# Gated cross-attention: the short path written out as one list, with scores issued further ahead, two buffers for two transposed operands, and one norm chain per batch

## What is computed

```
memory_proj = einsum('bme,de->bmd', memory, W_mem)
scores = einsum('bnd,bmd->bnm', x, memory_proj) / sqrt(D)
context = einsum('bnm,bmd->bnd', softmax(scores), memory_proj)
gate = sigmoid(einsum('bnf,df->bnd', concat([x, context]), W_gate) + b_gate)
x = rmsnorm(x + gate * context, norm_w)            # eps 1e-6
q = (layernorm(x) * ln_q_g + ln_q_b) @ Wq * 64 ** -0.5
k, v = split(ctx @ Wkv)
sim = where(media_mask, q @ k, -huge)              # 16 heads
x = x + tanh(attn_gate) * (softmax(sim) @ v) @ Wo
h = layernorm(x) * ln_ff_g + ln_ff_b
x = x + tanh(ff_gate) * gelu(h @ W1) @ W2
```

## Time and profile before

| | |
|---|---|
| median of 3 runs | 231.01 us (230.68 to 231.05) |
| profiled execution, its own time | 232.58 us |
| its span in the trace | 230.7 us |
| PE busy | 212.7 us (92%) |
| PEld busy | 170.0 us (74%) |
| DVE, ACT, POOL busy | 141.8, 127.4, 79.5 us |

### The profile page before, as it was taken

The page is one execution under the profiler, slowest core; times in us unless marked ns, Lnnn a source line. Parts: engine busy times, 40 slices in busy tenths (PEclk is TensorE's granted clock), DMA queues, the critical chain, the costliest instruction groups (busy, mean ns, idle before and its releaser), DMA issues.

```text
span 230.7 us, 4263 instructions
## 1 busy us (share of the span) xinstructions
PE 212.7 (92%) x1520; PEld 170.0 (74%) x1520; DVE 141.8 (61%) x296; ACT 127.4 (55%) x414; POOL 79.5 (34%) x82
## 2 busy tenths in 40 slices
PE   7769997998999999999999977999989999999994
PEld 4546544766976978976989855778867788998993
DVE  1575997635885556985655887867875567125410
ACT  3365754747457646567636466575449775028600
POOL 2030143943175333266331447636373007000000
PEclk9999997999999999999999999999999999999999
DMA  6984005050000000000000000050000000110011
GB/s 203 351 300 149 0 0 182 3 185 0 0 3 0 3 1 1 3 1 0 3 0 4 0 0 0 3 182 0 3 1 3 1 0 4 47 45 0 4 47 53
DMA packets 8463, 10.30 MB, mean 45 GB/s; under 512 B 754, under 2 KB 7668, under 8 KB 8052
## 3 DMA queue, kind: packets, MB, share of 16 engines
q1 hardware_dynamic: 7908, 9.71, 12.3%
q10 hardware_dynamic: 528, 0.26, 0.4%
HBM read 8.92 MB, written 1.05 MB: 43 GB/s over the span
## 4 chain that ended last, share of the span: by engine, by line
PE 56%; issue 13%; DVE 11%; POOL 10%; ACT 9%; POOLq 0%; ACTq 0%; DVEq 0%
PE bank L379 33%; ACT expd L585 6%; POOL probs L481 5%; PE bank L1080 4%; PE bank L1171 4%; PE bank L1050 3%; PE bank L1027 3%; PE bank L1090 3%; DVE neg_max L784 2%; PE bank L1229 2%; POOL wo_pair L519 1%; DVE probsT L797 1%; PE bank L1116 1%; PE bank L1134 1%; PE bank L1126 1%
## 5 line engine op out<-in xcount | busy, mean ns | idle before, releaser
L585 ACT ACTIVATE expd<-bank,neg_max 128x128 f32<-128x128 f32 (+1 forms) x136 | 50.5, 396 | 38.1 <-DVE neg_max L784 38.0
L481 POOL TENSOR_TENSOR probs<-expd,row_rcp 128x512 f32<-128x512 f32 x40 | 42.3, 1069 | 69.8 <-DVE row_rcp L792 63.2
L784 DVE TENSOR_REDUCE neg_max<-bank 128x4 f32<-128x512 f32 (+1 forms) x40 | 25.7, 683 | 6.0 <-PE bank L1050 3.6
L585 ACT ACTIVATION_READ_ACCUMULATOR expd<-bank,neg_max 128x1 f32 x136 | 29.3, 216 | 0.0
L379 PE MATMUL bank<-xhT_pair,wq_pair 128*128 128x256 f32 x192 | 27.5, 293 | 1.1 <-DVE fused L806 1.1
L379 PEld LDWEIGHTS bank<-xhT_pair,wq_pair 128*128 128x128 f32 x192 | 24.6, 194 | 5.0 <-DVE fused L806 1.9
L379 PE MATMUL bank<-wo_pair,oT_pair 128*128 128x256 f32 x192 | 26.6, 288 | 0.0
L1080 PE MATMUL bank<-ident,probs 128*128 128x128 f32 x160 | 22.6, 277 | 3.7 <-POOL probs L481 3.5
L379 PEld LDWEIGHTS bank<-wo_pair,oT_pair 128*128 128x128 f32 x192 | 23.6, 189 | 1.8
L1080 PEld LDWEIGHTS bank<-ident,probs 128*128 128x128 f32 x160 | 17.7, 140 | 8.4 <-POOL probs L481 7.1
L379 PE MATMUL bank<-wq_pair,gelu_pair 128*128 128x256 f32 x192 | 23.2, 281 | 0.4 <-issue 0.3
(11 more groups left out here) (125 smaller groups left out, 346.9 us busy)
## 6 DMA issues: line engine op xcount, KB each, us to landing
stage<-in_L_xattn_W_dram SPq DMA_DIRECT2D x2, 1024.0 KB, 5.0
x_sb<-in_x_dram SPq DMA_DIRECT2D x4, 256.0 KB, 8.7
wkv_sb<-in_L_xattn_Wkv_dram SPq DMA_DIRECT2D x1, 1024.0 KB, 9.2
stage<-in_L_xattn_Wq_dram SPq DMA_DIRECT2D x1, 1024.0 KB, 10.3
stage<-in_L_xattn_Wo_dram SPq DMA_DIRECT2D x1, 1024.0 KB, 5.4
out_dram<-x_sb SPq DMA_DIRECT2D x8, 128.0 KB, 1.7
ctx_sb<-in_ctx_dram SPq DMA_DIRECT2D x1, 768.0 KB, 7.1
probs<-in_L_xattn_W_gate_dram SPq DMA_DIRECT2D x1, 512.0 KB, 5.2
```

Of the source, the lines that this page charges most:

```text
L481: nc.gpsimd.tensor_tensor(probs[:, r, :].rearrange("p (h k) -> p h k", h=hb), expd[:, r, :].rearrange("p (h k) -> p h k", h=hb), row_rcp[: ...
L585: last = nc.scalar.activation(expd[:, r, h * w:(h + 1) * w], SC[n % 2][:, h * w:(h + 1) * w], ACT.Exp, bias=neg_max[:, r, h:h + 1], accum_ ...
L784: nc.vector.tensor_reduce(neg_max[:, r, 0:hb], SC[n % 2][:, :].rearrange("p (h k) -> p h k", h=hb), AX_X, ALU.max, negate=True).then_inc(d ...
```

## The change

The short path no longer comes from `body`: `HOT_KEYS` lists all its steps behind the branch. `PROLOGUE` is shorter: the branch now stands directly behind `y 1` and `flag`, before the first `gate`. `scores head u+1` and `u+2` are issued ahead of `av u`. `xT_pair` and `ctx_probsT` get an even and an odd copy. The two powers of POOL become one: `rms` multiplies by `norm_w` without `rms_r`, takes statistics, and forms `ms` and `ve = ms * LN_EPS + var` side by side in `squares`; one POOL power gives `rms_r` and `rstd`; POOL scales x by `rms_r` afterwards (`pool["x1"]`), beside the path to `xhT`. `ln_q_g` goes into the split of Wq (`lnq_cols`), and `ln_q_b @ Wq` becomes a vector `q_bias`, computed once on PE (`qbias`) and added where DVE copies `q`. Each `k` is now copied whole, by ACT and DVE in turn. The feed-forward part is the same but for its place.

```diff
-        for b in range(B):
-            if nt > 1:
+HOT_KEYS = (
+    ("splitq", 0), ("gate", 0), ("scores", "ctx", 1, 0), ("xT", 2), ("exp", "ctx", 1, 0), ("k", "hot", 0),
...
+        xT_pairs = [sb("xT_pair_even", [P, 2, K, N], F32R)]
+        ctx_probsTs = [sb("ctx_probsT_even", [P, KT, N])]
...
+            for i, v in enumerate((lnq_g, lnq_b)):
+                load(lnq_cols[:, i, :], v.rearrange("(p k) -> p k", k=K), w_in["lnq"])
             load_x(1)
...
+            sp.wait_ge(pe["qbias"], 1)
             load(stage[:, :].rearrange("p (i n) -> p i n", n=D), wo.rearrange("(i p) n -> p i n", p=P), w_in["wo"])
...
-                        if b:
-                            sc.wait_ge(pe["gate"], T * b)
+                        if b > 1:
+                            sc.wait_ge(pe["gate"], T * (b - 1))
...
+                    elif st[0] == "xhat":
+                        rows = x_sb[:, st[1] * T:(st[1] + 1) * T, :]
+                        gp.wait_ge(dve["xhat"], c)
+                        gp.wait_ge(pool["rstd"], c)
+                        nc.gpsimd.tensor_tensor(
+                            rows, rows, rms_r.rearrange("p (t a) -> p t a", a=1).to_broadcast([P, T, D]),
+                            ALU.mult).then_inc(pool["x1"], 1)
...
+                        ve_.wait_ge(w_in["lnq"], 32)
+                        nc.vector.tensor_scalar(lnq_cols[:, :, :], lnq_cols[:, :, :], DH ** -0.5, None, ALU.mult
+                                                ).then_inc(dve["lnq"], 1)
...
-                        nc.vector.tensor_copy(q_sb[:, 2 * j:2 * j + 2, :],
-                                              path.bank(st)[:, :].rearrange("p (i n) -> p i n", i=2)
-                                              ).then_inc(dve["q"], 1)
+                        shift = q_bias[:, 2 * j:2 * j + 2].rearrange("p (i a) -> p i a", a=1)
+                        nc.vector.tensor_tensor(q_sb[:, 2 * j:2 * j + 2, :],
+                                                path.bank(st)[:, :].rearrange("p (i n) -> p i n", i=2),
+                                                shift.to_broadcast([P, 2, N]), ALU.add).then_inc(dve["q"], 1)
...
+                    elif kind == "qbias":
+
+                        te.wait_ge(w_in["wq"], 16)
+                        te.wait_ge(dve["lnq"], 1)
+                        free(path, st)
+                        for pair in range(PAIRS):
+                            for k in range(K):
+                                last = nc.tensor.matmul(
+                                    path.bank(st)[:, pair:pair + 1], stage[:, k * INNER + pair * P:k * INNER + (pair + 1) * P],
+                                    lnq_cols[:, 1, k:k + 1], start=k == 0, stop=k == K - 1)
+                        last.then_inc(pe["qbias"], 1)
                     elif kind in ("xhT", "h2T"):
-                        te.wait_ge(pool["affine"], c if kind == "xhT" else B + c)
+                        if kind == "xhT":
+                            te.wait_ge(dve["xhat"], c)
```

223 lines of the change are left out of this document (129 added, 94 removed), and 6 rows, old and new, of the table HOT_KEYS.

## The result

The changed kernel takes 222.79 us in the median of four runs (221.95 to 226.74), the kernel before 230.88 us (230.68 to 231.05) beside it. The ratio is 0.9647 with a 95% interval of 0.9604 to 0.9690. Forecast were 224.4 us, range 221.0 to 228.8.

The account below looks back on a forecast made before the run. TensorE (PE), busy 212.7 of 230.7 us, was taken as the bound. From the 231.0 us median, −13.3 (waits) − 0.6 (`xT 1` moved) + 3.5 (`qbias`) + 1.3 (branch) + 2.5 (remaining waits) gave 224.4 us, range 221.0 to 228.8.

Parts of the forecast that it names:

- the sum: For the whole kernel, terms −13.3 − 0.6 + 3.5 + 1.3 + 2.5 give −6.6 us: 224.4 us.
- both families of waits: PE's waits for `probs` and for `xhat`, predicted to go: 9.2 us idle plus 4.1 us hidden, 13.3 us.
- The drain of 4.1: Beside its idle time, PE's waits were estimated to hide 4.1 us counted as busy: 15 times 0.27 us.
- (4): Waits of PE that the new order leaves over the 205 us behind the branch: adds 2.5 us.
- (1): One-column query-bias matmuls on PE, behind `v` and ahead of `xhT`, each pass with its weight load: adds 3.5 us.
- I take no cover: The query bias stands on PE's path with no wait for `xhat` hiding any of its 3.5 us.
- the 9.2: PE's idle us in the old kernel, from 17.8 us to its last matmul at 227.3, counted as removable.
- (2): Branch behind `y 1`: PE has nothing to do until the flag is loaded, delaying `gate 0` by 1.3 us.
- (3): Bias in DVE's `q` copy, whole `k` copies, POOL's `x1` pass, two tiny DMAs, Wo's later load: priced at nothing.
- (5): Granted clock may dip at the branch hole or `qbias`: one dip like before, its 1.6 us kept.
- the first rival: PE's clock stays up, without a dip: 1.6 us less, 222.8 us; chance 0.30.
- The crowded stretch: From 128.9 to 178 us PE keeps 5.06 us idle and a third more drain: 228.7 us; chance 0.14.

Follow-up runs that it names:

- e11: Changed kernel with scores of head units (2,1), (2,2) and (2,3) moved directly behind the spread of the unit before: 236.87 us.
- e5: Changed kernel with the steps behind the branch in the old kernel's order, `qbias` ahead of `xhT 0`: 244.39 us.
- e7: Changed kernel with the query norm's multiply and add back on POOL ahead of the transposes, and no query bias: 238.76 us.
- e4: Changed kernel with `tiles` and `flag` directly behind `ctxT 1` and `xT 1` ahead of `ctxT 3`, so the flag comes earlier: 222.41 us.
- e1: Changed kernel with only 4 of the 32 query-bias passes, the rest of the bias left out: 222.32 us.
- e6: Changed kernel with single buffers for transposed x and context probabilities, x transposes behind the gate that frees the buffer, `y 1` behind gate 0: 231.85 us.
- e3: Changed kernel with every head unit's scores, exponentials and normalisation behind the spread of the unit before, one unit ahead instead of two: 268.43 us.
- e2: Changed kernel with the query-bias matmuls done twice: 233.61 us.
- e8: Changed kernel with the flag made earlier as in e4, but `xT 1` behind `ctxT 3`: 222.61 us.
- e9: As e1, with `k` 3, 4 and 5 moved ahead of `xhT 0` into the bias's place: 222.12 us.
- e12: As e8, with the query bias cut into four groups of 8 passes between `k` and `v` steps: 221.14 us.

## Why the prediction was right, step by step

- **Where the time was.** The full-clock change is 9.3 us. PE's idle time fell by 7.5 (18.0 to 10.5). PE's busy time at full clock fell from 211.1 (229.1 less 18.0) to 209.3, with 3.5 us of bias added: another 5.3 us went. I take these for the hidden waiting, but they are a remainder, and no run separates them from other causes or from the error of the measure. The forecast's terms for these were 6.0 (9.2 + 0.6 − 1.3 − 2.5) and 4.1. So **"the sum"** of −6.6 was 2.7 too small, in the same direction in both.
- **"So both families of waits should go": right**, and shown to be the lead's work by e11 (7.4 us of waits come back where the lead is cut) and e5 (4.6 us with the old leads), and the fold's by e7 (14.2 us). The drain of 4.1 was an estimate from one place; the remainder of 5.3 is all that stands against it.
- **(4) "Waits that the new order leaves", 2.5 us: the largest miss.** Behind the branch they are 0.67 us. I had carried over the rate of the best old stretch; the new list has none of it.
- **(1) `qbias`, 3.5 us: the size right** (3.49 at full clock in e4, 109 ns each, as in the transposes). The Trainium skill (TensorE: Matmul & The Clock Gate, section LDWEIGHTS) gives a load as columns over 1.2, 107 ns; the distance from pass to pass agrees with it, while the rows record each load at 190 ns. **"I take no cover" was wrong**: leaving it out gives 1.2 us (e1). That PE's wait for `xhat` stands in its place had been counted as removed in the 9.2, so the sum was not hurt twice.
- **(2) The branch: a hole of 1.3 predicted, 1.74 measured.** The flag was formed by 21.21 us, a little earlier than the 21.35 taken; but from there to the first gate it took 1.29 us instead of 0.85, and the gate started at 22.5 instead of 22.2. Moving the flag gives 1.3 us back at a clock of 1.0 (e4).
- **(3) At nothing: right** for the bias add and POOL's power. The small DMAs and Wo's load, priced at nothing too, cause no wait of PE in the trace; the whole `k` copies were not taken back alone. For the second buffers I had no term of their own, and e6 shows 5.5 us that hang on them and on where `xT` may stand.
- **(5) The clock: one dip kept; none, one or two came.** Two of five executions show none, which is the first rival; the profiled one shows the two places named, the hole at the branch and the `qbias` stretch. Keeping the dip was also the wrong term for the median: 10 of 17 executions of before have a clock of 0.997 or more, so from the median of before a dip is added, not kept. The fall from median to median is the 9.3 us less some 1.2 of clock.
- **The number was met in part by luck.** 222.79 us is the first rival's 222.8, but for another reason: the clock did not stay up in the median execution, and where it did the time was 221.95 and 222.13. The gain was 2.7 us larger than the sum, and the clock took 1.2 of that back.
- **The other rivals did not come.** The crowded stretch lost 4.5 of its 5.06 us of idle time, PE does not wait for `exp` ahead of scores, and `qbias` keeps its 109 ns.
- **My experiments went wrong more than the forecast.** e3, e5, e6, e7 and e11 all lost more time than I expected. Taken back alone, the parts cost 5.5 (buffers), 8.2 (fold), 15.9 (order) and 32 us (lead), and together they bring 9.3. An order that leaves PE idle for only 2.4 us behind the first 17.8 was fitted to its own set of instructions. That this is why such prices do not add up to the gain is argued, not shown.

## What to carry to other kernels

In an order written out by hand, count for each dependent pair the work of the bottleneck engine that stands between its start and its use, and compare it with the measured latency: what is missing comes back as a wait of about that length (here 2.3 and 5.1 us for 3.6 and 4.6 counted), and may bring the clock down behind it. Move work into a place where the bottleneck engine waits for another engine anyway; here 3.05 us of it cost 1.2. A stretch of one-column matmuls may be worth cutting up among wide ones: here that cost about 0.4 us at full clock and gained 1.5 us in the median. And compare kernels at the same clock before comparing their medians.

## What was unexpected in the hardware

- The same program shows no fall of the granted clock in one execution and two in the next, and its spans go from 220.1 (clock 1.0) over 221.5 (0.992) to 224.9 us (0.975). Where the falls lie is known for the profiled executions alone. In the ones read here for it (before, after, e1, e2, e4, e8, e9 and e11) they follow holes in PE's work of 1.5 us and more, or lie in or behind a stretch of one-column matmuls. Yet the same hole of 1.7 us at the branch is followed by a fall in the profiled executions of after and e9, and by none in those of e1, e2 and e11.
- 64 one-column passes in a row (8.9 us) stand in a kernel whose clock fell in six of six executions, and in the profiled one it fell inside them, without a hole ahead. With 32 in a row it fell in three of five executions of after, four of six of e4 and all six of e8; with four groups of 8 in none of five (e12). But with 4 passes it fell in four of five of e1 (in the profile behind the 1.9 us hole that the bias had filled) and in four of six of e9, so the stretch is not the only cause. The Trainium skill (TensorE: Matmul & The Clock Gate, section on the HAM clock gate) says that the array's clock is held at the lower level unless activity releases it. The traces read here fit this as far as they go: the falls came behind holes, or in and behind the one-column stretch. In after the clock also fell at the branch, so e12 against after would not tell the hole from the stretch. e12 against e8 does better, since both have the flag early; but the fall of e8 in the slice from 11.1 to 16.6 us, behind a wait of 1.78 us that e12 has too, has nothing to do with the bias.
